# A decoder layer's self attention: the Newton steps of the layer norm's inverse root go from VectorE to GpSimd

## The chip, the cores and the metric

The kernel runs on one core of a Trainium2 chip. The metric is the device time of one execution in microseconds (us), as a median of several runs. Lower is better. The engines are TensorE (PE in the rows, PEld for its weight loads), VectorE (DVE), ScalarE (ACT), GpSimd (POOL) and SyncE (SP, here only a DMA queue).

## The reference, cut to what matters

The reference is one post-norm decoder layer on a batch of 8 sequences of 224 rows of 512: self attention, cross attention and a quantised feed-forward part, each followed by a residual add and a layer norm.

```
x = _layernorm(x + attn(rmsnorm(x)))     # 16 heads of 64, q and k normalised per head, scores soft-clamped by tanh
x = _layernorm(x + xattn(x, ctx))        # 16 heads, context of 750 rows of 384
x = _layernorm(x + ffn(x))
_layernorm(x) = (x - mean) / sqrt(var + 1e-5)      # over the 512 columns of a row
```

The layer norm behind self attention is the part that the change touches. Its inverse root is computed without a square root instruction: an integer shift and subtract give a first guess, and three Newton iterations refine it.

## The kernel before

Self attention takes its 16 heads in two groups of 8 (`g` = 0 and 1), and each group runs over the 8 sequences (`b`). One step of a group is a hand-written order of named pieces on each engine. A piece without a plus sign belongs to sequence b, one with a plus to b+1, one with two to b+2. The engines meet only by semaphores. A group's eight sequences are six steps in a loop, then steps written out; the last sequence of the second group is interleaved with the first pieces of cross attention by lists at the end of the file (`turn` on ACT, DVE and POOL, and a list of its own on PE).

The pieces that matter here are these.

- PE: `S1` to `S3` score pairs of heads, `O0` to `O7` multiply the values of one head by its weights, `Q0 K0 Q1 K1 V0 V1` project the next sequence, `T0` to `T3` transpose q and k, `Y0 Y1` project the output. `O4` waits for the low part of head 4's weights, and so on. `K1` goes to the PSUM bank that `Q0` leaves, so it waits until DVE has scaled `Q0` (line 729). `T0` waits for the scaled q and k of both halves (also line 729). The order on PE around them is: S1 O0 O1 S2 Q0+ O2 O3 K0+ S3 O4 O5 Q1+ O6 O7 K1+ V0+ Y0 T0+.
- ACT: exponentials, the high part `p_hi` of each head's weights (line 599), copies of the sums (lines 607 and 608), squares of projected rows (line 579).
- POOL: `P0` to `P7` subtract the high part from each head's weights, giving `p_lo` (line 392). `B0` to `B3` split the normalised output of a pair of heads into `o_hi` and `o_lo` (lines 398 and 400). Its order: P1 P2 P3 B0 P4 P5 P6 P7 B1 B2 B3, and then P0 of the next sequence.
- DVE: `I0` to `I3` invert the weight sums (`sa_sums`, line 751), `D0` to `D3` normalise the outputs with them (lines 758 and 759) and so free the bank and feed `B0` to `B3`. `HQ0` to `HK1` reduce squares per head (line 708). `N0.x` and `N1.x` are the inverse roots of the head norms, 12 dependent links each, after which q and k are scaled (line 729). `F0` to `F14` are the layer norm of the second group: F0 statistics (lines 778 and 779), F1 aggregation, F2 adds the epsilon, F3 and F4 make the guess (lines 1938 and 1940), F5 to F13 are the nine links of three Newton iterations on [112 x 2] elements, and F14 normalises the two halves of y (line 790), after which SP may store them.

DVE's order in a step ends with Y1, F0, T3+, XT0++, XT1++, F1 to F10, I0+, D0+, F11, F12, HQ0++, F13, F14, I1+, and the next step begins with HK0+, D1, N0.0+ and so on up to N0.11+, then Q0+.

Cross attention's second group has its own layer norm, and there the Newton iterations already run on POOL, in the form that the change brings to self attention: `refine_rsqrt` (lines 1384 to 1388), twelve dependent instructions on [112 x 2] in POOL's queue, between a wait for DVE's guess and a semaphore for which DVE's last link waits (line 1849).

Of the kernel before, what the change touches and what calls it, by code (L numbers as in the profile page):

```python
# [14 lines left out]
ALU = mybir.AluOpType  # L15
# [102 lines left out]
def self_attention(nc, ctx, at, psum, shared, x, norm_w, Wq, Wkv, Wo, q_gamma, k_gamma, acc, x1, ff_weights, ff_sum, ff_mean, ff_scale):  # L118
# [11 lines left out]
    LINKS = 1 + RSQRT_LINKS  # L130
    LN_LINKS = 3 + RSQRT_LINKS
    NW = len(ff_weights)
# [246 lines left out]
    def gpsimd(pool):  # L379
# [317 lines left out]
    def vector(dve):  # L697
# [116 lines left out]
        def values_lo(c, at):  # L814
# [3 lines left out]
            for t in range(2):  # L818
# [1721 lines left out]
```

## Time and profile before

| what | value |
|---|---|
| median of 3 runs | 1896.25 us (1895.83 to 1899.11) |
| the profiled execution | 1895.53 us, its span 1894.0 us |
| busy: PE, DVE, ACT, POOL over the span | 94%, 77%, 62%, 54% |
| self attention's second group, loop and unrolled steps | about 380 to 605 us of the span |
| one step of it | 35.36 us, PE busy 34.48 of them, DVE 30.53, ACT 22.81, POOL 14.25 |
| granted TensorE clock in that step | 1.00 of full speed |

Times in the rows count from the span's start. A row of the timeline is: start, length, engine, line, operation, output <- inputs with shapes, count; a bracket at the end is the idle time of the engine just before and what ended it. Neighbouring instructions of one group are merged ("x2"), and the length is then from the first start to the last end.

### The profile page before, as it was taken

The page shows a single profiled execution, that of the slowest core. Times are in us where ns is not written, and L with a number is a line of the kernel's source. Part 1 is how long each engine was busy: PE and PEld are TensorE (multiplying, and loading weights), DVE is VectorE, ACT ScalarE, POOL GpSimd, SP SyncE. Part 2 cuts the span into 40 slices and gives each one's busy share as a digit, 9 for nine tenths or more (in the row PEclk, how much of TensorE's full clock was granted, in tenths as well). Part 3 has the DMA queues.
Part 4 walks back from the last instruction along what each step waited for, and adds up shares of the span by engine and source line. Part 5 has one row for each costly group of instructions (what it writes and reads, how often), then busy time and mean ns, then how long its engine had stood idle before and what let it go on. Part 6 is the DMA issues. An engine that isn't in the chain of part 4 may idle for free.

```text
span 1894.0 us, 43077 instructions
## 1 busy us (share of the span) xinstructions
PE 1785.3 (94%) x14154; PEld 1492.8 (79%) x14154; DVE 1464.7 (77%) x3382; ACT 1181.4 (62%) x2696; POOL 1024.4 (54%) x1161
## 2 busy tenths in 40 slices
PE   5899998999999899999999999999999999979997
PEld 4777776777777788998998998899999999964443
DVE  5667667788888777787787788878777877778887
ACT  5675777566566565666665666566566656655664
POOL 0343343334434257766766744578778778542554
PEclk9899999999999899999999999999999999989999
DMA  3322233101103334324324333233313331271221
GB/s 121 116 85 72 74 104 107 40 29 39 48 29 120 98 99 127 102 93 144 99 67 144 118 132 91 58 93 91 110 55 107 90 110 47 67 161 41 67 66 61
DMA packets 109574, 166.80 MB, mean 88 GB/s; under 512 B 32488, under 2 KB 67672, under 8 KB 109512
## 3 DMA queue, kind: packets, MB, share of 16 engines
q1 hardware_dynamic: 91016, 129.77, 22.3%
q0 software_dynamic: 14656, 28.92, 5.5%
q10 hardware_dynamic: 3840, 7.34, 1.3%
q8 instruction: 33, 0.54, 0.1%
q14 instruction: 29, 0.24, 0.0%
HBM read 109.25 MB, written 50.46 MB: 84 GB/s over the span
## 4 chain that ended last, share of the span: by engine, by line
PE 58%; DVE 16%; issue 9%; DMA 6%; ACT 5%; POOL 4%; SPq 1%; POOLq 0%; DVEq 0%; ACTq 0%
PE att_ps_P L1524 5%; PE att_ps_SA L1548 5%; PE att_ps_P L1512 4%; PE att_ps_P L1573 3%; PE att_ps_T L1512 3%; PE att_ps_T L451 3%; PE att_ps_O L1512 3%; PE att_ps_T L1524 3%; PE att_ps_P L1562 3%; PE att_ps_O L1524 3%; DVE sa_sums L751 2%; PE att_ps_P L1584 2%; PE att_ps_SB L513 2%; PE att_ps_T L1573 2%; DMA out_dram<-ff_y_out 2%
## 5 line engine op out<-in xcount | busy, mean ns | idle before, releaser
L1360 POOL TENSOR_TENSOR ca_pr<-ca_pr,ca_rec 112x750 f32<-112x750 f32 x256 | 370.1, 1466 | 218.8 <-DVE ca_rec L1799 215.8
L392 POOL TENSOR_TENSOR sa_p_lo<-sa_pr,sa_p_hi 112x448 fp32r<-112x448 f32 x128 | 148.0, 1162 | 330.9 <-ACT sa_p_hi L599 330.9
L1689 ACT ACTIVATE ca_big<-att_ps_P 126x384 fp32r<-126x384 f32 (+1 forms) x256 | 105.7, 448 | 69.2 <-PE att_ps_P L1562 67.8
L751 DVE RECIPROCAL sa_sums<-sa_sums 128x224 f32<-128x224 f32 x64 | 99.2, 1550 | 46.7 <-ACT sa_sums L608 46.3
L1683 ACT ACTIVATE ca_pr<-att_ps_SA,ca_nmax 112x750 f32<-112x750 f32 x128 | 113.6, 888 | 20.0 <-DVE ca_nmax L1795 9.5
L1804 DVE TENSOR_TENSOR ca_big<-att_ps_P,ca_big 126x384 fp32r<-126x384 f32 (+1 forms) x256 | 120.1, 497 | 4.4 <-ACT ca_big L1689 4.1
L1795 DVE TENSOR_REDUCE ca_nmax<-att_ps_SA 112x1 f32<-112x752 f32 x128 | 119.1, 930 | 0.4 <-PE att_ps_SA L1548 0.4
L1795 DVE TENSOR_REDUCE ca_nmax<-att_ps_SB 112x1 f32<-112x752 f32 x128 | 118.9, 929 | 0.0
L1524 PE MATMUL att_ps_P<-ca_w_hi,ca_ct 128*126 128x256 f32 x576 | 118.2, 284 | 0.0
L1683 ACT ACTIVATE ca_pr<-att_ps_SB,ca_nmax 112x750 f32<-112x750 f32 x128 | 113.1, 884 | 0.0
L1573 PE MATMUL att_ps_P<-ca_big,ca_v_st 126*128 126x448 f32 x378 | 90.9, 376 | 8.3 <-DVE ca_big L1804 8.3
L451 PE MATMUL att_ps_T<-sa_w_hi,sa_xt_hi 128*112 128x512 f32 x192 | 82.6, 430 | 16.3 <-DVE sa_qs L729 10.7
L1562 PEld LDWEIGHTS att_ps_P<-att_ident,ca_pr 64*126 64x126 f32 (+1 forms) x1536 | 85.5, 138 | 14.8 <-issue 10.3
L1562 PE MATMUL att_ps_P<-att_ident,ca_pr 48*126 48x48 f32 (+1 forms) x1536 | 92.6, 223 | 4.5 <-DVE ca_q_lo L1778 2.2
L1548 PE MATMUL att_ps_SA<-ca_k_hi,ca_q_hi 64*112 64x376 f32 x256 | 94.3, 368 | 2.2 <-ACT ca_pr L1683 2.2
L1524 PEld LDWEIGHTS att_ps_P<-ca_w_hi,ca_ct 128*126 128x126 f32 x576 | 94.0, 187 | 2.2
L1548 PE MATMUL att_ps_SB<-ca_k_hi,ca_q_hi 64*112 64x376 f32 x256 | 94.0, 367 | 0.0
L1401 POOL TENSOR_SCALAR ca_stage<-ca_stage 128x688 f32<-128x688 f32 x36 | 90.5, 2513 | 3.1
L499 PE MATMUL att_ps_SB<-sa_p_hi,sa_v_hi 112*128 112x224 f32 x256 | 77.5, 303 | 11.5 <-POOL sa_p_lo L392 10.9
L1548 PE MATMUL att_ps_SA<-ca_k_hi,ca_q_lo 64*112 64x376 f32 x256 | 85.3, 333 | 0.0
L1548 PE MATMUL att_ps_SB<-ca_k_hi,ca_q_lo 64*112 64x376 f32 x256 | 85.2, 333 | 0.0
L1548 PE MATMUL att_ps_SA<-ca_k_lo,ca_q_hi 64*112 64x376 f32 x256 | 85.2, 333 | 0.0
(342 smaller groups left out, 6653.5 us busy)
## 6 DMA issues: line engine op xcount, KB each, us to landing
ct_kept<-ca_ct SPq DMA_DIRECT2D x8, 1134.0 KB, 9.2
ca_ct<-ct_kept POOLq DMA_DIRECT2D x8, 1134.0 KB, 8.1
ct_kept<-ca_ct SPq DMA_DIRECT2D x8, 1116.0 KB, 12.0
ca_ct<-ct_kept POOLq DMA_DIRECT2D x8, 1116.0 KB, 10.1
sa_xin<-in_x_dram SPq DMA_DIRECT2D x16, 448.0 KB, 3.8
xt_kept<-ca_xt SPq DMA_DIRECT2D x8, 896.0 KB, 5.3
ca_xt<-xt_kept POOLq DMA_DIRECT2D x8, 896.0 KB, 5.0
ternary<-ca_stage SPq DMA_DIRECT2D x36, 172.0 KB, 1.9
```

Of the source, the lines that this page charges most:

```text
L392: pool.tensor_tensor(p_lo[:, h % NB, :], pr[:, h % NB, :], f32(p_hi[:, h % NB, :]), ALU.subtract).then_inc(p_split, 1)
L451: mm = pe.matmul(ps(u)[0:R, :], xs[:, k, c * R:c * R + R], ws[i][:, k, :], start=(n == 0), stop=(n == len(passes) - 1))
L751: dve.reciprocal(sums[:, p % 2, :], sums[:, p % 2, :]).then_inc(inverted, 1)
L1360: pool.tensor_tensor(w, w, rec[:, h % PB, c:c + 1].to_broadcast([R, S]), ALU.mult).then_inc(norm_done, 1)
L1512: mm = pe.matmul(st(u).bank[:, 0:SH], ws[:, k, p * P:p * P + P], cs[:, k, a * S1:a * S1 + SH], start=(n == 0), stop=(n == len(todo) - 1))
L1524: mm = pe.matmul(st(u).bank[0:J, 0:VC], cs[:, k, J0[j]:J0[j] + J], ws[:, k, vh * VC:vh * VC + VC], start=(n == 0), stop=(n == len(todo) - 1))
L1548: mm = pe.matmul(psum[scores_slot(h)][0:R, BANK * half:BANK * half + SH], qs[of, p, c * R:c * R + R], ks[of, p, half * S1:half * S1 + SH], ...
L1562: mm = pe.transpose(to.bank[0:J, j * width:j * width + width], pr[rows, h % PB, c, J0[j]:J0[j] + J], ident[rows, rows])
L1573: mm = pe.matmul(to.bank[:, 0:2 * N], v_st[0:JN[j], j, h, :], big[0:JN[j], h % 2, j, :, :].rearrange("s l n -> s (l n)"), start=(j == 0), ...
L1683: act.activation(pr[:, h % PB, c, :].rearrange("r (a s) -> r a s", a=2), two_halves(psum[slot]), ACT.Exp, bias=nmax[:, h % PB, c:c + 1], a ...
L1795: dve.tensor_reduce(nmax[:, h % PB, c:c + 1], both, AX.XY, ALU.max, negate=True).then_inc(max_done, 1)
L1804: dve.tensor_tensor(weights_view(h, c, x, True), blocks_view(source.bank, x), f32(weights_view(h, c, x, False)), ALU.subtract).then_inc(so ...
```

## The change

1. The nine Newton links leave DVE. DVE keeps F0 to F4 (statistics, epsilon, guess); the new F5 is the old F14, and it first waits for `rs_done`.
2. POOL gets a piece `L`: it waits for `guess_done`, runs twelve [112 x 2] instructions, each waiting for the one before, and raises `rs_done`. Where DVE fused a multiply and an add in one instruction, POOL uses two. `rs_begun` is raised on the way; nobody in self attention waits for it.
3. In POOL's order the loop body is cut at another place: P1, P2, P3 and B0 of a sequence now stand at the end of the body before. The sequence of instructions is the same in the loop except that L stands between P3 and B0. In the last sequence, B0 moves from behind P5 to ahead of P4, and the last L stands behind B3.
4. In DVE's order, I0 and D0 come right behind F4, then HQ0, then F5, then I1. In the closing list the same is done for the last two sequences: I0 and D0 ahead of the norm's last link for sequence 6, and K00, K01 ahead of it for sequence 7.
5. The variance with epsilon and the scratch tile lie in SBUF instead of PSUM, since POOL works on them.

```diff
-    LN_LINKS = 3 + RSQRT_LINKS
+    LN_LINKS = 5
...
-        ORDER = steps("""P1 P2 P3 B0 P4 P5 P6 P7 B1 B2 B3 P0+""")
+        ORDER = steps("""P4 P5 P6 P7 B1 B2 B3 P0+ P1+ P2+ P3+ L B0+""")
+        rs_chain = Chain(pool, rs_own, 3 * 4)
+
+        def refine_rsqrt(b):
+            rs_chain.step(counter(b, 0, B))
+            pool.wait_ge(guess_done, counter(b, 0, B)(1, 1))
+            pool.sem_inc(rs_begun, 1)
+            for n in range(3):
+                rs_chain.link(pool.tensor_tensor(ln_newton[:, :], mv[:, :, 1], rs[:, :], ALU.mult))
+                rs_chain.link(pool.tensor_tensor(ln_newton[:, :], ln_newton[:, :], rs[:, :], ALU.mult))
+                pool.sem_inc(rs_begun, 1)
+                rs_chain.link(pool.tensor_scalar(ln_newton[:, :], ln_newton[:, :], -0.5, 1.5, ALU.mult, ALU.add))
+                rs_chain.link(pool.tensor_tensor(rs[:, :], rs[:, :], ln_newton[:, :], ALU.mult))
+            pool.sem_inc(rs_done, 1)
...
-            elif link < LN_LINKS:
-                rsqrt_link(dve, link - 3, ln_var, rs[:, :], ln_newton).then_inc(ln_own, 1)
+            elif link == 3:
+                rsqrt_link(dve, 0, mv[:, :, 1], rs[:, :], ln_newton[:, :]).then_inc(ln_own, 1)
+            elif link == 4:
+                rsqrt_link(dve, 1, mv[:, :, 1], rs[:, :], ln_newton[:, :]).then_inc(guess_done, 1)
             else:
+                dve.wait_ge(rs_done, at(1, 1))
                 for c in range(2):
                     dve.tensor_scalar(y[:, c, :], y[:, c, :], mv[:, c, 0:1], rs[:, c:c + 1], ALU.subtract, ALU.mult).then_inc(y_done, 1)
...
-                   V1+ T1+ T2+ G++ Y1 F0 T3+ XT0++ XT1++ F1 F2 F3 F4 F5 F6 F7 F8 F9 F10 I0+ D0+ F11 F12 HQ0++ F13 F14 I1+""")
+                   V1+ T1+ T2+ G++ Y1 F0 T3+ XT0++ XT1++ F1 F2 F3 F4 I0+ D0+ HQ0++ F5 I1+""")
...
-            turn("""P1 P2 P3 P4 P5 B0 P6 B1 P7 B2 B3 N0.0+ ...
+            turn("""P4 P5 P6 B1 P7 B2 B3 L N0.0+ ...
...
-            turn("""E0 w0+ w1+ E1 E2 E3 E4 E5 E6 E7 E8 E9 E10 E11 E12 E13 E14 I0 D0 I1 D1 ... Y1 F0 Q0+ F1 F2 F3 F4 F5 K00+ F6 F7 F8 F9
-                    F10 K01+ F11 F12 F13 F14 M0.0+ ...
+            turn("""E0 w0+ w1+ E1 E2 E3 E4 I0 D0 E5 I1 D1 ... Y1 F0 Q0+ F1 F2 F3 F4 K00+ K01+ F5 M0.0+ ...
```

(The E pieces of the last list are the F pieces of sequence 6, done under another letter.)

## Rows read from the trace of the kernel before

**Rows 1.** What PE waited for, 390 to 620 us: total, times, longest.
```profile
PE att_ps_SB L499 <- POOL sa_p_lo L392: 4.0, 2, 2.2
PE att_ps_T L451 <- DVE sa_qs L729: 3.4, 6, 0.8
PE att_ps_P L468 <- DVE sa_qs L729: 1.6, 6, 0.3
```

**Rows 2.** Timeline of PE in one step: O4, O5, Q1, O6, O7, K1, T0.
```profile
473.50 0.37 PE L499 MATMUL att_ps_SB<-sa_p_hi,sa_v_hi 112*128 112x224 f32 x1
...
474.27 0.27 PE L499 MATMUL att_ps_SB<-sa_p_hi,sa_v_hi 112*128 112x224 f32 x1
...
474.94 0.40 PE L451 MATMUL att_ps_P<-sa_w_hi,sa_xt_hi 128*112 128x512 f32 x1
...
478.27 0.27 PE L499 MATMUL att_ps_SB<-sa_p_hi,sa_v_lo 112*128 112x224 f32 x1
478.62 0.37 PE L499 MATMUL att_ps_SB<-sa_p_hi,sa_v_hi 112*128 112x224 f32 x1
...
480.07 0.48 PE L451 MATMUL att_ps_T<-sa_w_hi,sa_xt_hi 128*112 128x512 f32 x1 [0.52 <-DVE sa_qs L729]
...
488.95 0.41 PE L468 MATMUL att_ps_P<-att_ident,sa_qs 112*128 112x112 f32 x2 [0.29 <-DVE sa_qs L729]
```

**Rows 3.** Timeline of POOL in the same step: P3, B0 (two rows), P4, P5.
```profile
467.66 1.15 POOL L392 TENSOR_TENSOR sa_p_lo<-sa_pr,sa_p_hi 112x448 fp32r<-112x448 f32 x1 [0.63 <-ACT sa_p_hi L599]
469.70 0.56 POOL L398 TENSOR_TENSOR sa_o_hi<-sa_o,att_zero 128x224 fp32r<-128x224 f32 x1 [0.89 <-DVE sa_o L759]
470.34 0.67 POOL L400 TENSOR_TENSOR sa_o_lo<-sa_o,sa_o_hi 128x224 fp32r<-128x224 f32 x1
470.97 1.39 POOL L392 TENSOR_TENSOR sa_p_lo<-sa_pr,sa_p_hi 112x448 fp32r<-112x448 f32 x1
472.55 1.15 POOL L392 TENSOR_TENSOR sa_p_lo<-sa_pr,sa_p_hi 112x448 fp32r<-112x448 f32 x1 [0.19 <-ACT sa_p_hi L599]
```

**Rows 4.** Timeline of DVE in the same step: F4, HQ0, F14, I1.
```profile
465.90 0.16 DVE L1940 TENSOR_SCALAR sa_rs<-att_ps_O 112x2 int32<-112x2 int32 x1
...
469.87 0.69 DVE L708 TENSOR_REDUCE att_ps_O<-sa_sq 112x8 f32<-112x512 f32 x1
...
470.80 1.85 DVE L790 TENSOR_SCALAR sa_y<-sa_y,sa_mv,sa_rs 112x512 f32<-112x512 f32 x2
472.56 1.54 DVE L751 RECIPROCAL sa_sums<-sa_sums 128x224 f32<-128x224 f32 x1
```

**Rows 5.** Timeline of POOL in cross attention: the same Newton pass, first, third and last link.
```profile
1284.84 0.19 POOL L1384 TENSOR_TENSOR ca_newton<-ca_mv,ca_rs 112x2 f32<-112x2 f32 x1 [1.01 <-DVE ca_rs L1940]
...
1285.50 0.19 POOL L1387 TENSOR_SCALAR ca_newton<-ca_newton 112x2 f32<-112x2 f32 x1 [0.20 <-POOL ca_newton L1385]
...
1288.20 0.20 POOL L1388 TENSOR_TENSOR ca_rs<-ca_rs,ca_newton 112x2 f32<-112x2 f32 x1
1288.64 0.67 POOL L1365 TENSOR_TENSOR ca_o<-ca_o,ca_tmp 128x224 f32<-128x224 f32 x1 [0.24 <-POOL ca_rs L1388]
```

**Rows 6.** Timeline of DVE behind that pass: the last link of the norm.
```profile
1289.17 1.24 DVE L1849 TENSOR_SCALAR ca_res<-ca_res,ca_mv,ca_rs 112x512 f32<-112x512 f32 x2
```

**Rows 7.** Timeline of POOL in the last sequence: P2 and P3, P4 and P5.
```profile
609.18 2.23 POOL L392 TENSOR_TENSOR sa_p_lo<-sa_pr,sa_p_hi 112x448 fp32r<-112x448 f32 x2 [4.33 <-ACT sa_p_hi L599]
612.47 2.24 POOL L392 TENSOR_TENSOR sa_p_lo<-sa_pr,sa_p_hi 112x448 fp32r<-112x448 f32 x2 [1.07 <-ACT sa_p_hi L599]
```

**Rows 8.** Timeline of PE in the last sequence: the last matmul of O5.
```profile
616.40 0.27 PE L499 MATMUL att_ps_SB<-sa_p_hi,sa_v_lo 112*128 112x224 f32 x1
```

**Rows 9.** The chain that ended last: start, length, what.
```profile
617.56 0.35 ACT sa_sums L607
...
642.60 1.01 DVE sa_y L790 x2
```

**Rows 10.** Timeline of DVE in the last norm: F4.
```profile
639.56 0.16 DVE L1940 TENSOR_SCALAR sa_rs<-att_ps_O 112x2 int32<-112x2 int32 x1
```

More of the change, by code:

```diff
@@ L265, in self_attention @@
     ln_own = sem("ln_own")
+    guess_done = sem("guess_done")
+    rs_begun = sem("rs_begun")
+    rs_own = sem("rs_own")
+    rs_done = sem("rs_done")
     ff_loaded = [sem(f"ff_loaded{m}") for m in range(NW)]
@@ L410, in step @@
             for name, n in ORDER:
-                if batches[n]:
+                if name == "L":
+                    if g and batches[n]:
+                        refine_rsqrt(b)
+                elif batches[n]:
                     do(name, batches[n][1])
@@ L420, in gpsimd, with last @@
                 step(b, g)
-        return lambda name: do(name, counter(B - 1, GROUPS - 1, B))
+        def last(name):
+            if name == "L":
+                refine_rsqrt(B - 1)
+            else:
+                do(name, counter(B - 1, GROUPS - 1, B))
+        return last
     def tensor(pe):
@@ L772, in layernorm_link @@
             at = counter(b, 0, B)
-            if link:
-                dve.wait_ge(ln_own, at(LN_LINKS, link))
+            if 0 < link < LN_LINKS:
+                dve.wait_ge(ln_own, at(LN_LINKS - 1, link))
             if link == 0:
@@ L784, in layernorm_link @@
             elif link == 2:
-                dve.tensor_scalar(ln_var, mv[:, :, 1], LN_EPS, None, ALU.add).then_inc(ln_own, 1)
-            elif link < LN_LINKS:
-                rsqrt_link(dve, link - 3, ln_var, rs[:, :], ln_newton).then_inc(ln_own, 1)
+                dve.tensor_scalar(mv[:, :, 1], mv[:, :, 1], LN_EPS, None, ALU.add).then_inc(ln_own, 1)
+            elif link == 3:
+                rsqrt_link(dve, 0, mv[:, :, 1], rs[:, :], ln_newton[:, :]).then_inc(ln_own, 1)
+            elif link == 4:
+                rsqrt_link(dve, 1, mv[:, :, 1], rs[:, :], ln_newton[:, :]).then_inc(guess_done, 1)
             else:
+                dve.wait_ge(rs_done, at(1, 1))
                 for c in range(2):
@@ L2453, in _ @@
             ff_first, ff_rest = ff.gpsimd(pool)
-            turn("""P1 P2 P3 P4 P5 B0 P6 B1 P7 B2 B3 N0.0+ N1.0+ N0.1+ N1.1+ N2.0+ N3.0+ N2.1+ N3.1+ B0+ N4.0+ N5.0+""", last, first)
+            turn("""P4 P5 P6 B1 P7 B2 B3 L N0.0+ N1.0+ N0.1+ N1.1+ N2.0+ N3.0+ N2.1+ N3.1+ B0+ N4.0+ N5.0+""", last, first)
             rest(ff_first)
@@ L2484, in _ @@
             last = sa.vector(dve)
-            turn("""E0 w0+ w1+ E1 E2 E3 E4 E5 E6 E7 E8 E9 E10 E11 E12 E13 E14 I0 D0 I1 D1 I2 D2 CT00+ XT0+ w2+ w3+ XT1+ I3 D3
-                    CT01+ w4+ w5+ total CT02+ w6+ CT10+ w7+ Y0 CT11+ CT12+ w8+ w9+ Y1 F0 Q0+ F1 F2 F3 F4 F5 K00+ F6 F7 F8 F9
-                    F10 K01+ F11 F12 F13 F14 M0.0+ M1.0+ K10+ R0.0+ R1.0+ K11+ Q1+ K20+ M0.1+ M1.1+ K21+ R0.1+ R1.1+ Q2+ w10+
+            turn("""E0 w0+ w1+ E1 E2 E3 E4 I0 D0 E5 I1 D1 I2 D2 CT00+ XT0+ w2+ w3+ XT1+ I3 D3
+                    CT01+ w4+ w5+ total CT02+ w6+ CT10+ w7+ Y0 CT11+ CT12+ w8+ w9+ Y1 F0 Q0+ F1 F2 F3 F4 K00+ K01+ F5 M0.0+ M1.0+ K10+ R0.0+ R1.0+ K11+ Q1+ K20+ M0.1+ M1.1+ K21+ R0.1+ R1.1+ Q2+ w10+
                     w11+ T0.0a+ T0.0b+ T1.0a+ T1.0b+ M2.0+ M3.0+ Q3+ V00+ R2.0+ V01+ R3.0+ w12+ V02+ w13+ V03+ T0.1a+ T0.1b+
```

3 lines of the change are left out of this document (1 added, 2 removed).

## The prediction

> **What bounds the kernel now.** I began with the page and the windows view of one step of the second group: PE is busy for 34.5 of a step's 35.4 us, so hardly a microsecond a step is to be won here, and the waits view says what it is. The reader is to see two gates of DVE in it [rows 1]: in each of six steps PE stands for 3.4 / 6 = 0.57 us ahead of K1 and for 1.6 / 6 = 0.27 us ahead of T0, both times for rows scaled at line 729. The third row is POOL's p_lo, and its two waits, 4.0 us together, lie in the last sequence, not in the loop. So in the loop a shorter DVE can give back 0.57 + 0.27 = 0.84 us a step at the very most, and POOL costs PE almost nothing there as yet. What that "nothing" rests on is the next view: the timeline of the four engines over one step, PE in [rows 2], POOL in [rows 3], DVE in [rows 4]. P4 is done at 470.97 + 1.39 = 472.36 and O4 starts at 473.50, so head 4's low part has 1.14 us to spare. P5 is done at 472.55 + 1.15 = 473.70 and O5 starts at 474.27: 0.57 us to spare. O7 has none: it starts 0.35 us after the matmul before it, where the pitch of these matmuls is 0.11 us, so it already waits some 0.24 us.
>
> **What the change takes from DVE.** Nine links of [112 x 2], six ahead of I0 and three around HQ0. F4, an instruction of the same size, took 0.16 us [rows 4], so they are 9 x 0.16 = 1.4 us of DVE's queue a step, and a little more with the gaps between dependent links. It counts only if I1, HK0 and the N0 chain behind them really start earlier, and that is decided by when the new F5 may run.
>
> **What it puts on POOL, and when.** The pass's price has a row: the same twelve instructions on the same shape in cross attention run from 1284.84 to 1288.20 + 0.20 = 1288.40, which is 3.56 us, and POOL's next instruction follows 0.24 us later [rows 5]. L stands behind P3. P3 waits for ACT's high part of head 3, which the change doesn't move, and ends at 467.66 + 1.15 = 468.81 [rows 3]. The guess has been there since about 466.1 [rows 4], so the wait for it costs nothing, and the pass begins one wait and one semaphore increment later, 0.20 us by the gap ahead of line 1387 [rows 5]: 469.0. It ends at 472.6, and B0 starts at 472.8 instead of 469.70, 3.1 us late. That is the step on which everything turns: P3 is the wrong neighbour, because P4 and P5 are due within 5 us of it and B0 must go first.
>
> **The path over POOL and PE.** B0 takes 1.27 us to P4's start (469.70 to 470.97) [rows 3]; in cross attention the instruction behind the pass took 0.67 us, so I allow B0 up to 1.5. P4 then starts at 474.1 to 474.3 and ends 1.15 later at 475.3 to 475.5; P5 ends at 476.4 to 476.7. O4 can't start at 473.50 but at 475.4, and O5 not before 476.5 to 476.7 instead of 474.27: 2.2 to 2.4 us late, and Q1 with it. Of that O7's 0.24, K1's 0.57 and T0's 0.27 are swallowed, as these waits end later anyway: 2.3 - 1.1 leaves 1.1 to 1.4 us a step on this path alone.
>
> **The path over DVE.** F5 stands where the old F14 stood, ahead of I1, and it now waits for the pass: about 472.8 against 470.80, 2.0 us late. Behind it in DVE's queue are I1, HK0, D1 and the N0 chain, back to back up to Q0's scaling, which is K1's gate. F5's own length matters too. Before, the pair took from 470.80 to 472.56, 1.76 us, with POOL in P4; the last sequence's pair took 1.01 with POOL idle [rows 9], and cross attention's pair, which runs beside the same neighbours on POOL as F5 will, took 1.24 [rows 6]. So I1 starts at 474.0 (by the cross attention row) to 474.5 (by the 1.76) instead of 472.56: 1.4 to 2.0 us late, and K1 and then T0 with it. The nine links saved are used up in the wait. The row nearest to the case is cross attention's, so I take 1.5 us a step for the larger of the two paths; they run side by side and don't add.
>
> The pair of line 790 shows two engines in each other's way: 1.85 us beside P4, 1.01 alone, and P4 itself 1.39 instead of 1.15 [rows 3, 4, 9]. The Trainium skill (GPSIMD Engine Reference, Key points) says that GpSimd shares its SBUF interfaces with VectorE, with contention when VectorE works in a two-port mode or reads two SBUF inputs. By that rule moving work of VectorE's to GpSimd also makes the rest meet more often; if F5 met P4 again I would take the upper end, 2.0 us a step, and the sum would be 3 us more. The trace agrees with the rule in the rows just named; it doesn't change which path decides.
>
> **The number of steps.** F and L of sequences 0 to 5 fall into such steps: six, as many as the waits in [rows 1]. 6 x 1.5 = 9.0 us (6.6 to 12.0).
>
> **Sequence 6, in the crossing to cross attention.** P2 and P3 end at 609.18 + 2.23 = 611.41 [rows 7]. The pass follows, 611.6 to 615.2; B0, now ahead of P4, takes 615.4 to about 616.8; P4 ends at 617.9 and P5 at 619.1, where before both were done by 612.47 + 2.24 = 614.71. O5 ended at 616.40 + 0.27 = 616.67 [rows 8] and now starts at 619.1, ending at 619.8 to 620.4 (the upper end if the clock is low, as it was shortly before). ACT's copy of that pair's sums began at 617.56 and is a piece of the chain that ended last [rows 9]; it now begins at 619.9 to 620.4. So 2.3 to 2.9 us, and I take 2.6. The sooner I0 and D0 don't help, since B0 stands behind the pass.
>
> **Sequence 7, the last norm.** DVE's guess ends at 639.56 + 0.16 = 639.7 [rows 10], POOL is idle, and the pass takes 639.9 to 643.5. The closing pair starts at 643.6 instead of 642.60, and it too lies on the chain that ended last [rows 9], ahead of the store that cross attention's next loads queue behind: 1.0 us. Zero if those loads have slack that the chain doesn't show.
>
> **At nothing.** The cut of POOL's loop at another place changes no order in the first group, and P1 to P3 wait for ACT wherever the cut is. SBUF in place of PSUM for the [112 x 2] tiles touches F2 and F3, which are ahead of I0 and no longer than F4's 0.16 us each [rows 4]; even at half that, more or less, DVE has time there, since it must wait for the pass afterwards. The store of y comes 1.4 to 2.0 us later, and y is needed again only by Y0's add, which is behind T0's gate at 488.95 [rows 2], some 16 us after the pair's end: only a delay of that size would use up the cover.
>
> **The sum.** 9.0 + 2.6 + 1.0 = 12.6 us. Against the profiled execution's 1895.53 that is 1908.1; the median of the runs shown is 0.7 higher than that execution, so the forecast for a median is 1908.8.
>
> **The rivals.**
>
> *VectorE's relief decides (faster).* If L were done early enough, F5 would follow HQ0 directly, at 469.87 + 0.69 = 470.6 or sooner [rows 4], K1's wait would vanish and perhaps part of T0's: up to 0.84 x 6 = 5.0 us, so 1891 to 1894. For it speaks that PE does wait for DVE in each step and that DVE is without a pause from its Y1 add to T0's gate. Against it: it needs `rs_done` by 470.6, and P3 alone ends at 468.81. The pass would have to take under 1.8 us, half of what [rows 5] shows. Chance 0.05.
>
> *It is hidden (no change).* The delays on POOL and DVE might meet slack I count wrongly, for example if PE catches up by other pieces, and only the ends remain: 2 to 3 us, 1896 to 1899. Against it: PE has 0.9 us of idle in a step, and P5's slack is 0.57 us against 3 us of delay. Chance 0.07.
>
> *Only the path over POOL counts, and the ends are covered.* 6 x 1.1 with little else: 1902 to 1905. Chance 0.13, and it lies at the lower edge of my range.
>
> *It costs more.* F5 meets P4 again, PE's clock falls to its lower level in the longer pauses of the crossing, and that stretch grows by several us: 6 x 2.0 + 2.9 + 1.0 and 2 to 4 for the clock, 1914 to 1917. The granted clock of the windows around 600 to 650 us is already the lowest of the stage. Chance 0.10.
>
> **How the numbers follow.** The forecast has 0.65: 1905 to 1914 with 6.6 to 12.0 for the steps and 2.3 to 3.9 for the ends. Range 1902 to 1914, which leaves out the rivals of the first two kinds and most of the last. A measurement of this kernel tells 0.2%, 3.8 us, from no change. Faster by more 0.04, within 0.09, slower 0.87.
>
> **What will show it.** Right: in a step of the second group, L's first link 0.2 us behind P3 and 3.56 us long; B0 3.1 us later against P3; new rows for PE at line 499 waiting for p_lo at O4 and O5, some 2.3 us a step; the DVE pair of line 790 preceded by idle time ended by POOL; step length near 36.9 us. K1's wait stays or grows although DVE is less busy by at least 1.4 us a step. Wrong: step length 34.5 to 35.4 and no wait at O4. The prediction fails if POOL's pass is far from 3.56 us here, or if P4 and P5 are not what PE waits for.

## The result, and the profile after

The changed kernel takes 1914.49 us (median of 4 runs, 1913.83 to 1918.05) against 1897.24 us (4 runs beside it, 1895.83 to 1899.11): ratio 1.009, 95% interval 1.0074 to 1.0106. It is slower by 17.25 us; 12.6 us were forecast, and the time lies 0.5 us above the range given. One execution of the filled version below ran at a granted clock of 0.65, took 2466 us and is left out of its ratio.

Where PE waits, first: the view that answers to [rows 1], 390 to 640 us (total, times, longest).

```profile
PE att_ps_SB L524 <- POOL sa_p_lo L408: 16.4, 13, 3.0
```

Both gates of DVE are gone from the list, and what is left is POOL's p_lo. The timeline of PE in one step (the one whose P3 starts at 473.86) shows where; the rows are the last of S3, the first of O4 and of O5, the last two of O5, the first two of Q1, two of Q1 behind the turn of the clock, and the first of O6, K1 and T0. [rows 2] has most of them for the kernel before.

```profile
479.51 0.27 PE L507 MATMUL att_ps_SA<-sa_q_hi,sa_k_lo 64*112 64x224 f32 x2
481.52 0.37 PE L524 MATMUL att_ps_SB<-sa_p_hi,sa_v_hi 112*128 112x224 f32 x1 [1.75 <-POOL sa_p_lo L408]
...
482.63 0.37 PE L524 MATMUL att_ps_SB<-sa_p_hi,sa_v_hi 112*128 112x224 f32 x1 [0.18 <-POOL sa_p_lo L408]
...
483.23 0.41 PE L524 MATMUL att_ps_SB<-sa_p_lo,sa_v_hi 112*128 112x224 f32 x1
483.45 0.41 PE L524 MATMUL att_ps_SB<-sa_p_hi,sa_v_lo 112*128 112x224 f32 x1
483.66 0.63 PE L476 MATMUL att_ps_P<-sa_w_hi,sa_xt_hi 128*112 128x512 f32 x1
484.09 0.63 PE L476 MATMUL att_ps_P<-sa_w_lo,sa_xt_hi 128*112 128x512 f32 x1
...
486.59 0.40 PE L476 MATMUL att_ps_P<-sa_w_lo,sa_xt_hi 128*112 128x512 f32 x1
486.82 0.39 PE L476 MATMUL att_ps_P<-sa_w_hi,sa_xt_lo 128*112 128x512 f32 x1
...
487.74 0.27 PE L524 MATMUL att_ps_SB<-sa_p_hi,sa_v_hi 112*128 112x224 f32 x1
...
489.08 0.40 PE L476 MATMUL att_ps_T<-sa_w_hi,sa_xt_hi 128*112 128x512 f32 x1
...
497.64 0.41 PE L493 MATMUL att_ps_P<-att_ident,sa_qs 112*128 112x112 f32 x2
```

Two things are to be seen. PE stands for 1.75 us ahead of O4, as forecast. And behind that pause the distance from one 128x512 matmul to the next is 0.43 us (483.66 to 484.09) instead of 0.23 (486.59 to 486.82): the clock fell from 2.4 to 1.2 GHz at about 483.1, since the last two matmuls of O5 are already 0.22 us apart where the pitch was 0.11, and it came back at about 486.4. The fall is there in all six steps. Q1 takes 487.74 - 483.66 = 4.08 us, where it took 477.72 - 474.94 = 2.78 us before. The windows view, 400 to 600 us, says the same for all steps (columns: time, then busy us of PE, PEld, DVE, ACT and POOL, the granted clock, DMA); the first row is of the kernel before.

```profile
400.00:600.00 200.00, 194.57 (x1251) 151.41 (x1249) 173.00 (x467) 124.74 (x283) 80.05 (x91) 1.00 0.14 43
```

```profile
400.00:600.00 200.00, 188.05 (x1168) 147.02 (x1168) 155.91 (x389) 121.17 (x276) 89.19 (x156) 0.95 0.13 39
```

POOL and DVE in the same step, answering to [rows 3] and [rows 4]: P3, first and last link of the pass, B0, then P4 to P6 in one row; below it the guess's last instruction (F4), HQ0, the pair F5 and I1.

```profile
473.86 1.16 POOL L408 TENSOR_TENSOR sa_p_lo<-sa_pr,sa_p_hi 112x448 fp32r<-112x448 f32 x1 [0.64 <-ACT sa_p_hi L624]
474.98 0.20 POOL L399 TENSOR_TENSOR sa_ln_newton<-sa_mv,sa_rs 112x2 f32<-112x2 f32 x1
...
478.34 0.19 POOL L403 TENSOR_TENSOR sa_rs<-sa_rs,sa_ln_newton 112x2 f32<-112x2 f32 x1
478.85 0.73 POOL L414 TENSOR_TENSOR sa_o_hi<-sa_o,att_zero 128x224 fp32r<-128x224 f32 x1 [0.32 <-POOL sa_rs L403]
479.66 0.72 POOL L416 TENSOR_TENSOR sa_o_lo<-sa_o,sa_o_hi 128x224 fp32r<-128x224 f32 x1
480.34 3.34 POOL L408 TENSOR_TENSOR sa_p_lo<-sa_pr,sa_p_hi 112x448 fp32r<-112x448 f32 x3
```

```profile
472.11 1.14 DVE L1968 TENSOR_SCALAR sa_rs<-sa_ln_newton 112x2 int32<-112x2 int32 x1
...
475.56 0.69 DVE L733 TENSOR_REDUCE att_ps_O<-sa_sq 112x8 f32<-112x512 f32 x1
478.62 1.25 DVE L818 TENSOR_SCALAR sa_y<-sa_y,sa_mv,sa_rs 112x512 f32<-112x512 f32 x2 [2.36 <-POOLq L404]
479.78 1.54 DVE L776 RECIPROCAL sa_sums<-sa_sums 128x224 f32<-128x224 f32 x1
```

The pass takes 478.53 - 474.98 = 3.55 us, and from P3's start to B0's it is 4.99 us instead of 2.04. A step, measured between equal rows of two steps, has 37.88 us instead of 35.36: +2.52. Over the whole second group, from P3 of sequence 0 (398.09, before 396.94) to P0 of sequence 7 (618.45, before 602.59), it is 220.36 - 205.65 = 14.7 us.

The ends: Y0's add of the last sequence, and the last pair of the norm, with the kernel before in the first fence.

```profile
633.26 0.69 DVE L768 TENSOR_TENSOR sa_y<-att_ps_SB,sa_res 112x512 f32<-112x512 f32 x1 [1.84 <-PE att_ps_SB L513]
```

```profile
652.06 0.69 DVE L793 TENSOR_TENSOR sa_y<-att_ps_SB,sa_res 112x512 f32<-112x512 f32 x1 [0.93 <-PE att_ps_SB L538]
...
662.38 1.00 DVE L818 TENSOR_SCALAR sa_y<-sa_y,sa_mv,sa_rs 112x512 f32<-112x512 f32 x2 [1.48 <-POOLq L404]
```

P2 of sequence 7 starts at 625.54 (609.18 in [rows 7]), so from there to Y0's add it is 26.52 us instead of 24.08: +2.4, forecast 2.6. From Y0's add to the pair it is 10.32 instead of 9.34 [rows 9]: +1.0, forecast 1.0. Between the two stretches, from P0 to P2 of sequence 7, lie 7.09 us instead of 6.59, +0.5; cross attention's first weights are on the chain there and land 7.3 us behind their issue instead of 6.8. 14.7 + 0.5 + 2.4 + 1.0 = 18.6 us. The two profiled executions are 22.5 us apart, since the changed one is 3.6 us above its median and the one of before 1.7 below the median beside it; of the 3.9 us left, 1.15 lie ahead of P3 of sequence 0 and the rest behind the last norm; their cause is open.

The +2.4 agree with the forecast in part by luck. The copy of sums that the forecast followed starts 637.26 - 625.54 = 11.72 us behind P2, where it was 617.56 - 609.18 = 8.38: 3.3 us late, not 2.3 to 2.9; O4 and O5 ran at 1.2 GHz behind a pause of 3.01 us and took 2.9 us together. Up to Y0's add 0.9 us of it were caught up.

### The profile page after: what moved, and what is told of

It reads as the page before. It is cut to its first block, busy times and chain, and to the rows that moved or that the text cites. A ratio compares the mean times of both kernels' runs of the same rounds, so it can differ in the third digit from the quotient of the medians.

```text
span 1916.5 us, 43151 instructions
## 1 busy us (share of the span) xinstructions
PE 1791.7 (93%) x14128; PEld 1500.8 (78%) x14154; DVE 1455.7 (76%) x3310; ACT 1181.6 (62%) x2696; POOL 1041.8 (54%) x1257
## 4 chain that ended last, share of the span: by engine, by line
PE 52%; issue 15%; DVE 9%; POOL 9%; DMA 8%; ACT 5%; SPq 1%; POOLq 1%; DVEq 0%; ACTq 0%
PE att_ps_SA L1576 5%; PE att_ps_P L1552 5%; PE att_ps_P L1540 4%; PE att_ps_P L1601 3%; PE att_ps_O L1540 3%; PE att_ps_T L1540 3%; DMA ca_ct<-ct_kept 3%; PE att_ps_T L1552 3%; PE att_ps_P L1590 2%; POOL sa_p_lo L408 2%; PE att_ps_O L1552 2%; PE att_ps_P L1612 2%; PE att_ps_T L476 2%; PE att_ps_T L1601 2%; DMA out_dram<-ff_y_out 2%
```

## The experiments

Each was timed beside the kernel before on the same chip. Medians of the kernel before were 1895.6 us beside the first four runs below, 1897.6 beside the two smaller passes, Q1 ahead of O4 with the pass, and the split pass, 1896.7 beside the four from the pass in GpSimd's idle time to the filling without a pause, and 1896.9 beside the pair moved alone and Q1 ahead of O4 without the pass. "Step" is the length of one step of the second group in the profile.

**GpSimd's pass alone.** VectorE keeps its code; GpSimd does twelve instructions of the same kind on tiles of its own, in the changed kernel's order.

```
-        ORDER = steps("""P1 P2 P3 B0 P4 P5 P6 P7 B1 B2 B3 P0+""")
+        ORDER = steps("""P4 P5 P6 P7 B1 B2 B3 P0+ P1+ P2+ P3+ L B0+""")
...
+                rs_chain.link(pool.tensor_tensor(own_newton[:, :], own_var[:, :], own_rs[:, :], ALU.mult))
```

> VectorE as before the change, with all its Newton links; GpSimd has the twelve instructions behind P3 too, on tiles of its own, and nobody waits for their result. Theory: the loss of a step comes over GpSimd, which hands head 4's and 5's low parts to TensorE about 2 us late; TensorE then pauses and runs at its lower clock for some 3 us behind the pause. It expects O4's pause of 1.7 to 1.8 us, the low clock behind it, a step of 37.5 to 38 us instead of 35.36 and 1909 to 1914 us. Rival 1, the loss comes from VectorE's wait for rs_done: no pause ahead of O4 that costs anything in the end, a step of 35.4 to 36 and 1896 to 1900 us.

Measured: 1916.33 us, ratio 1.0101 (1.0087 to 1.0114), step 37.7 us, granted clock 0.95. The timeline of PE, O4:

```profile
481.28 0.56 PE L523 MATMUL att_ps_SB<-sa_p_hi,sa_v_hi 112*128 112x224 f32 x1 [1.99 <-POOL sa_p_lo L413]
```

The whole loss is there with none of VectorE's waits for GpSimd: I1 starts 4.23 us behind P3 here, earlier than in the kernel before. The path over POOL is enough for it. The pass took 4.02 us and not 3.55, and B0 to P4 1.25 and not 1.49, so O4 comes 0.2 us later than in the changed kernel.

The steps of this trace aren't equal: 36.54, 37.72, 37.70, 39.21 and 38.11 us, with a pause of 1.97 to 2.00 us ahead of O4 in each. The rows show the first and the fourth: O4's first matmul and two neighbours of Q1 behind it.

```profile
407.02 0.37 PE L523 MATMUL att_ps_SB<-sa_p_hi,sa_v_hi 112*128 112x224 f32 x1 [1.97 <-POOL sa_p_lo L413]
...
409.13 0.39 PE L475 MATMUL att_ps_P<-sa_w_lo,sa_xt_hi 128*112 128x512 f32 x1
409.36 0.39 PE L475 MATMUL att_ps_P<-sa_w_hi,sa_xt_lo 128*112 128x512 f32 x1
```

```profile
518.98 0.56 PE L523 MATMUL att_ps_SB<-sa_p_hi,sa_v_hi 112*128 112x224 f32 x1 [1.99 <-POOL sa_p_lo L413]
...
522.11 0.63 PE L475 MATMUL att_ps_P<-sa_w_lo,sa_xt_hi 128*112 128x512 f32 x1
522.54 0.63 PE L475 MATMUL att_ps_P<-sa_w_hi,sa_xt_lo 128*112 128x512 f32 x1
```

In the first step the matmuls behind the pause stay 0.23 us apart. The clock didn't fall, and the step is 1.18 us longer than the 35.36 before: that is the price of the delay alone. In the fourth the slow stretch lasts from O4 to 525.5, some 6.5 us, and the step is 2.67 us longer than the first. One kernel, the same pause, and the step's length goes with the stretch at 1.2 GHz.

**VectorE's relief alone.** No pass, no Newton iteration; the pair waits for the guess only.

```
-                dve.wait_ge(rs_done, at(1, 1))
+                dve.wait_ge(guess_done, at(1, 1))
```

> The Newton iterations are left out altogether: the norm is scaled with the first guess. VectorE has the new short order, GpSimd has no pass. All theories expect a gain, since this is the most that VectorE's relief can be worth: TensorE's waits for VectorE ahead of K1 (0.57 us) and T0 (0.27 us) go, a step of 34.5 to 34.9 us, 1891 to 1894 us. If the relief is worth nothing even then, 1896 to 1898 us and a step of 35.3.

Measured: 1896.88 us, ratio 1.0008 (0.9998 to 1.0018), step 35.27 us. A miss: 1.4 us less on VectorE gave back 0.09. The timeline of DVE (the guess's last instruction, the pair, I1) and of POOL (P2, P4) says why.

```profile
465.34 1.17 DVE L1968 TENSOR_SCALAR sa_rs<-sa_ln_newton 112x2 int32<-112x2 int32 x1
...
469.55 2.28 DVE L818 TENSOR_SCALAR sa_y<-sa_y,sa_mv,sa_rs 112x512 f32<-112x512 f32 x2
471.75 1.54 DVE L776 RECIPROCAL sa_sums<-sa_sums 128x224 f32<-128x224 f32 x1
```

```profile
465.33 1.16 POOL L408 TENSOR_TENSOR sa_p_lo<-sa_pr,sa_p_hi 112x448 fp32r<-112x448 f32 x1 [2.54 <-ACT sa_p_hi L624]
...
470.21 1.34 POOL L408 TENSOR_TENSOR sa_p_lo<-sa_pr,sa_p_hi 112x448 fp32r<-112x448 f32 x1
```

An instruction on 112 x 2 elements took 1.17 us and ended with P2, and the pair ended 0.3 us behind P4. What the nine links had cost went into waiting beside POOL: 1.0 us at the guess's last instruction and 0.4 at the pair (2.28 instead of 1.85), so VectorE's busy time between 400 and 600 us is 173.4 us, where it was 173.0 before.

**VectorE's wait alone.** As in the last run, without pass and Newton links, but the pair also waits for the low part of head 4 of the next sequence, so it is late and GpSimd isn't.

```
+                if not isinstance(b, int) or b < B - 1:
+                    dve.wait_ge(p_split, counter(b, 1, B, 1)(HG, 5))
```

> As the run without iterations, but VectorE's last link of the norm waits for head 4's low part of the next sequence, which is ready at about the moment at which rs_done came, while GpSimd has no pass in its way. So only VectorE is late. The theory (GpSimd's lateness and the clock) expects no pause ahead of O4, and ahead of K1 1.5 to 1.8 us instead of 0.57: a step of 36.2 to 36.6 and 1901 to 1905 us if TensorE's clock stays up behind that pause. If the clock falls behind any pause of this length, 2.5 us a step and 1911 or more. Rival 1 (VectorE's wait carries the loss) expects 1911 to 1915 us too, but with the full clock in the rows.

Measured: 1903.33 us, ratio 1.004 (1.0027 to 1.0053), step 35.85 us, clock 0.99. PE, K1 and T0:

```profile
480.58 0.49 PE L476 MATMUL att_ps_T<-sa_w_hi,sa_xt_hi 128*112 128x512 f32 x1 [0.96 <-DVE sa_qs L754]
...
489.47 0.41 PE L493 MATMUL att_ps_P<-att_ident,sa_qs 112*128 112x112 f32 x2 [0.30 <-DVE sa_qs L754]
```

The path over VectorE exists, and costs 0.5 us a step here. K1's wait is 0.96 us and not the 1.5 to 1.8 expected, because this edit holds VectorE back less than the pass does: I1 starts 5.21 us behind P3, 0.31 later than in the kernel before, where the changed kernel has 5.92. So the run doesn't price that path at its full length. Its sixth step comes nearer: there the pair met P5 and took 1.84 us, I1 starts 6.04 us behind P3, K1 waits 1.96 us, the clock is low for some 3.4 us behind it, and the step is 37.73 us instead of 35.41. By that one step (2.3 us) the path over VectorE, left to itself, might cost nearly as much as the path over POOL; no run tests it. In the changed kernel K1 and T0 don't wait at all, so it is hidden there. The six steps add up to 4.8 us more than before, the medians are 7.7 apart, and the profiled execution was the fastest of the five; the rest isn't explained.

**Filling the pause.** The changed kernel with six useless 128x512 matmuls between S3 and O4, into a bank that is free until Q1 writes it.

```
                     do(name, batches[n][1])
+                    if name == "S3" and g and batches[1]:
+                        keep_busy(batches[1][1])
```

> The changed kernel, and TensorE does six useless 128x512 matmuls into Q1's free bank between S3 and O4 in the second group, about 1.4 us in the pause that it has there (1.4 us more work a step in all, whose result is overwritten). Theory: the granted clock stays at full speed behind the pause, O5 and Q1 lose their extra 1.6 us, of which K1's gate gives about 1.3 back: a step of 36.4 to 36.9 us instead of 37.88, 1904 to 1909 us. If the clock has nothing to do with the pause, the same 1914 us or up to 8 us more.

Measured: 1909.11 us, ratio 1.0066 (1.0053 to 1.0079), step 36.55 us, clock 1.00. PE at O4 and O5:

```profile
479.07 0.37 PE L529 MATMUL att_ps_SB<-sa_p_hi,sa_v_hi 112*128 112x224 f32 x1 [0.20 <-POOL sa_p_lo L408]
480.18 0.37 PE L529 MATMUL att_ps_SB<-sa_p_hi,sa_v_hi 112*128 112x224 f32 x1 [0.18 <-POOL sa_p_lo L408]
```

PE does more and the step is 1.33 us shorter. O4 comes no earlier (7.70 us behind P3, in the changed kernel 7.66); what went is the stretch at 1.2 GHz. T0 now waits 0.26 to 0.28 us for VectorE again, so without the low clock the two paths end close together.

**Two iterations, and one.** The pass with `range(2)` and `range(1)` for `range(3)`, and the count of links to match.

> The changed kernel with two of the three Newton iterations in GpSimd's pass (the iterate is less exact, so the outputs differ a little; nothing else is left out). The pass should take 2.35 us instead of 3.5, B0 start 1.2 us earlier and P4 end 0.6 to 0.8 us after the end of S3, where it now is 1.75 us late. Theory A (the delay in front of O4 and the lower TensorE clock behind it are two terms, and the clock term comes only with a long pause): PE pauses 0.5 to 0.8 us at O4, the granted clock of the loop stays at 0.99 to 1.00, and the step is 35.5 to 35.9 us, that is 1896 + 1 to 4 = 1897 to 1900 us. Theory B (the loss is proportional to the delay, with no separate clock term): two thirds of the loss of the step stay, 37.0 us a step, and 1907 to 1909 us. The smaller loss of the ends (2.4 and 1.0 us, each less one iteration of 1.14 us) is in both.

Measured: 1898.17 us, ratio 1.0002 (0.9993 to 1.0012), step 35.36 us, clock 1.00.

```profile
470.55 0.37 PE L524 MATMUL att_ps_SB<-sa_p_hi,sa_v_hi 112*128 112x224 f32 x1 [0.54 <-POOL sa_p_lo L408]
```

> The changed kernel with one of the three Newton iterations in GpSimd's pass (less exact outputs again). The pass takes 1.15 to 1.2 us, B0 starts about 0.6 us later than in the kernel before, and P4 ends at about 473, inside the 1.14 us that O4 has to spare. Both theories: no pause at O4 and O5, clock 1.00, step 35.2 to 35.4 us, 1895 to 1898 us. If the step is still longer by more than 0.3 us, something besides the length of the pass costs time (the wait for the guess, the order of B0 and P4, F5 behind HQ0).

Measured: 1896.07 us, ratio 0.9995 (0.9983 to 1.0008), step 35.00 us, clock 1.00, no wait for p_lo in the steps.

So the loss isn't proportional to the pass: one iteration gives -0.36 us a step, two 0.0, three +2.5. From two to three, 1.2 us of POOL's time, 1.2 us go into the delay of O5 that nothing swallows any more and 1.3 into the clock.

**Q1 ahead of O4**, first with the pass, then in the kernel before.

```
-S3 O4 O5 Q1+ O6 O7 K1+
+S3 Q1+ O4 O5 O6 O7 K1+
```

> The changed kernel with PE's order S3 Q1 O4 O5 O6 O7 K1 instead of S3 O4 O5 Q1 O6 O7 K1: Q1 needs nothing of GpSimd and takes 2.78 us, so it stands in the pause of 1.75 us. Clock theory: no pause at O4, no fall of the clock, O4 to O7 back to back behind Q1 as far as the high and low parts of heads 6 and 7 allow it; what stays is VectorE's late gate of K1 and T0. Step 35.8 to 36.5 us (kernel before 35.36, changed kernel 37.88), granted clock 0.99 to 1.00, 1900 to 1904 us. Rival (the delay itself is the whole loss, wherever PE stands): PE waits at O6, O7 and K1 for as much as it did at O4 and O5, step 37 us or more, 1909 us or more.

> The kernel before with PE's order S3 Q1 O4 O5 O6 O7 K1, in both groups. If the order alone costs (ScalarE copies the sums of O4 and O5 ahead of the high part of head 7, P7 stands behind it on GpSimd, and O7 needs it), PE waits about 1.9 us at O7 in every step, the clock falls behind that, and the time is 1915 us or more. If it costs only together with GpSimd's pass, the step stays within 0.5 us of 35.36 and the time within 1894 to 1900 us.

Measured: 1926.02 us, ratio 1.0153 (1.0137 to 1.0169), step 37.5 us with the pass; 1920.68 us, ratio 1.012 (1.0103 to 1.0137), step 37.5 us without it. A miss. The second run says that the order costs by itself, so the first tells nothing of the pass. From the run without the pass, the timelines of ACT (the first copy of the sums of O4 and O5, head 7's high part), POOL (P7) and PE (O7, and K1 behind it):

```profile
491.01 0.36 ACT L607 ACTIVATE sa_sums<-att_ps_SB 64x224 f32<-64x224 f32 x1 [1.93 <-PE att_ps_SB L499]
...
491.76 0.58 ACT L599 ACTIVATE sa_p_hi<-sa_pr 112x448 fp32r<-112x448 f32 x1
```

```profile
492.42 1.13 POOL L392 TENSOR_TENSOR sa_p_lo<-sa_pr,sa_p_hi 112x448 fp32r<-112x448 f32 x1 [2.11 <-ACT sa_p_hi L599]
```

```profile
493.60 0.37 PE L499 MATMUL att_ps_SB<-sa_p_hi,sa_v_hi 112*128 112x224 f32 x1 [1.96 <-POOL sa_p_lo L392]
...
494.68 0.63 PE L451 MATMUL att_ps_T<-sa_w_hi,sa_xt_hi 128*112 128x512 f32 x1
495.11 0.63 PE L451 MATMUL att_ps_T<-sa_w_lo,sa_xt_hi 128*112 128x512 f32 x1
```

With O4 and O5 behind Q1, ScalarE's sums come late, the high part of head 7 stands behind them in its queue, P7 behind that, and PE meets the same kind of pause at O7, with the same fall of the clock behind it.

**The pass split.** One iteration behind P3, two behind P5 of the next step, the pair behind K0's scaling.

```
+        ORDER = steps("""P4 P5 M P6 P7 B1 B2 B3 P0+ P1+ P2+ P3+ L B0+""")
...
+I2 N0.11+ Q0+ K0+ F5 D2 I3
```

> The pass split up and the pair moved: GpSimd does one iteration behind P3 (0.89 us of idle time there) and the other two behind P5 of the next step (2.36 us of idle time there in the kernel before); VectorE's closing pair of the norm moves from ahead of I1 to behind the scaling of Q0 and K0 in the next step, behind K1's gate. If the place of the pass is what costs, then P4 ends about 0.5 us later than before and within O4's slack, P6 and P7 come 0.5 to 0.7 us late, O7 0.45 us late, and K1's wait of 0.57 and T0's of 0.27 us are swallowed or gone, since I1 starts 1.2 us earlier: step 34.9 to 35.3 us, no pause over 0.6 us, clock 1.00. With about 1 us of loss in the last norm: 1893 to 1897 us. If GpSimd's pass costs wherever it stands (contention with VectorE, P6 and P7 late), the step is 35.6 us or more and the time 1899 us or more.

Measured: 1903.24 us, ratio 1.0029 (1.0017 to 1.0042), step 35.9 us, clock 1.00. A miss in the step: no wait for p_lo, but one for T0's rows.

```profile
495.46 0.41 PE L503 MATMUL att_ps_P<-att_ident,sa_qs 112*128 112x112 f32 x2 [1.21 <-DVE sa_qs L764]
```

From Q0's scaling to the last scaling ahead of T0 VectorE hasn't a pause, and a pair of 0.99 us put into that stretch comes out as 0.9 us more wait.

**The pass where GpSimd idles.** All twelve instructions behind B3 of the next step, the pair behind the last scaling of K1's rows, Y0's add behind V1.

```
+        ORDER = steps("""P4 P5 P6 P7 B1 B2 B3 M P0+ P1+ P2+ P3+ B0+""")
...
+Q1a+ K1a+ Q1b+ K1b+ F5 T0+ V0+ V1+ Y0 T1+
```

> The whole pass of twelve instructions moved to where GpSimd idles: behind B3 of the next step (idle for 10 us there), the closing pair on VectorE behind the last scaling of the Q1 and K1 rows (1.16 us of idle time there), Y0's add one place later (behind V1), and the guess's intermediate back in PSUM. In the crossing the pass of sequence 6 stands between B2 and B3 (3.95 us idle), its pair behind D3. If place alone decides, there is no wait for p_lo in the steps, I1 starts when ScalarE's sums are there (4.24 us behind P3's start instead of 4.90), and the step is 34.8 to 35.1 us, clock 1.00: 1892 to 1896 us, the last norm still costing 1.0. If moving the pair towards T0 costs as in the split version (its pair lay wholly on T0's path), step 35.6 us or more and 1899 us or more.

Measured: step 35.02 us, clock 1.00, but 1903.3 us, ratio 1.004 (1.0025 to 1.0054). The step came out as expected, the total didn't. POOL's pass (first and last link) and DVE's pair, then the waits of PE, 390 to 640 us:

```profile
484.97 0.20 POOL L402 TENSOR_TENSOR sa_ln_newton<-sa_mv,sa_rs 112x2 f32<-112x2 f32 x1
...
488.34 0.20 POOL L406 TENSOR_TENSOR sa_rs<-sa_rs,sa_ln_newton 112x2 f32<-112x2 f32 x1
```

```profile
488.62 1.00 DVE L829 TENSOR_SCALAR sa_y<-sa_y,sa_mv,sa_rs 112x512 f32<-112x512 f32 x2
```

```profile
PE att_ps_P L1536 <- DVE ca_ct L1820: 4.1, 1, 4.1
PE att_ps_P L1521 <- DMA ca_xin<-x: 3.9, 1, 3.9
```

The full pass costs next to nothing in a step if it stands here: the run with only the pair moved has 34.84. The loss is in the crossing: the store of sequence 5 now stands late in SP's queue, and cross attention's first loads behind it. The first weights, issued at 598.13, land 10.69 us later, where it was 6.8 us before. That this is the whole of the loss wasn't tested.

**Guess in PSUM, without and with the pass.** `ln_guess = norms[:, 4 * HN:4 * HN + 2]` for the guess's intermediate, as in the kernel before.

> As the version without pass and without Newton iterations (only the first guess, so the norm is not exact), but the guess's intermediate in PSUM as in the kernel before. There the last instruction of the guess, SBUF to SBUF, took 1.17 us beside P2, and the pair 2.28 us beside B0 and P4. Port theory: an instruction of VectorE's that goes from SBUF to SBUF waits for the end of GpSimd's instruction, one that reads PSUM doesn't: the guess's last instruction takes 0.16 us again, D0 and B0 come 1.0 us earlier, the pair meets less of P4 and takes 1.2 to 1.7 us, I1 starts at the time of ScalarE's sums, step 34.9 to 35.1 us (35.27 without PSUM), 1893 to 1896 us. Rival (the 1.17 us are a property of the instruction and not of where its source lies): 1.17 us stay, step 35.27, 1897 us.

Measured: 1894.9 us, ratio 0.9997 (0.9985 to 1.0008), step 35.03 us (35.27 with SBUF). DVE's instruction and POOL's P2 beside it:

```profile
464.60 0.16 DVE L1969 TENSOR_SCALAR sa_rs<-att_ps_O 112x2 int32<-112x2 int32 x1
```

```profile
464.58 1.16 POOL L409 TENSOR_TENSOR sa_p_lo<-sa_pr,sa_p_hi 112x448 fp32r<-112x448 f32 x1 [2.54 <-ACT sa_p_hi L625]
```

0.16 us beside P2 where SBUF to SBUF took 1.17. The pair still took 2.12 us, not the 1.2 to 1.7 expected: it meets P4 all the same.

> The changed kernel with nothing else altered than the guess's intermediate in PSUM instead of SBUF. The last instruction of the guess should take 0.16 instead of 1.14 us, with I0, D0 and HQ0 1.0 us earlier. The prediction put this placement at nothing, since VectorE has to wait for the pass anyway: then the pair starts at the same distance from P3, the step stays at 37.8 to 37.9 us, and the time at 1912 to 1916 us. If it counts after all (the guess or B0's source being late), the step is shorter by up to 1.0 us and the time lies near 1908 to 1910 us.

Measured: 1911.71 us, ratio 1.009 (1.0072 to 1.0108), step 37.53 us (37.88). The pair starts 4.76 us and I1 5.92 us behind P3's start in both kernels, so VectorE gained nothing, as the prediction had it. The 0.35 us are most likely the clock's: PE's second matmul of O4 already slows down here (0.36 us, then one every 0.21), and the slow stretch covers O5's wait of 0.18, while in the changed kernel it begins only within O5. The first step of this trace has no fall behind its pause of 1.77 us, as in the run with GpSimd's pass alone, and is 36.58 us long.

**The filling without a pause.** The same six matmuls in the kernel before.

> Control for the version with filling matmuls: the kernel before with the same six useless 128x512 matmuls (1.4 us a step) between S3 and O4. No pause there to hide them in. O4 to K1 come 1.4 us later, of which K1's wait of 0.57 and T0's of 0.27 us may swallow a part: step 35.9 to 36.8 us (35.36 without), clock 1.00, 1899 to 1905 us. If the matmuls were of use to the clock by themselves, and not only in the pause, the step would be about 35.4 us or less, 1896 us.

Measured: 1898.54 us, ratio 1.0012 (1.0000 to 1.0024), step 35.44 us, clock 1.00: 0.08 us more for 1.4 us of work. PE has no wait left between 390 and 590 us, so what K1, T0 and the small gaps at O4 to O7 had left idle took it in. A smaller cost than expected, and it gives the filled version its meaning: its 1.19 us over the kernel before are the late O5 and, at T0, VectorE, hardly the filling. The first step of the run with GpSimd's pass alone says the same without any filling: 1.18.

**Only the pair moved.** The kernel before, Newton links on VectorE, GpSimd untouched; the pair behind the last scaling of K1's rows (Z), Y0's add behind V1; sequences 5 and 6 as before.

```
+Q1a+ K1a+ Q1b+ K1b+ Z T0+ V0+ V1+ Y0 T1+
```

> The kernel before, all Newton links left on VectorE and GpSimd untouched; only the closing pair of the norm moved in the steps of the second group, from ahead of I1 to behind the last scaling of K1's rows in the next step (1.16 us of idle time there), with Y0's add one place later; sequences 5 and 6 keep the pair where it was. If the place of the pair is what VectorE can give back, I1 starts 4.24 us behind P3 (when ScalarE's sums are there) instead of 4.90, K1's wait of 0.52 to 0.57 us goes, and the step is 35.0 us (35.36 before) in five steps: 1894 to 1896 us, ratio 0.999. If relief of VectorE needs the Newton links gone as well, the step stays at 35.2 to 35.4 us.

Measured: step 34.84 us (35.36), but 1895.88 us, ratio 0.9992 (0.998 to 1.0004). DVE, I1:

```profile
470.19 1.55 DVE L751 RECIPROCAL sa_sums<-sa_sums 128x224 f32<-128x224 f32 x1 [1.13 <-ACT sa_sums L608]
```

I1 now waits for ScalarE's sums, 4.24 us behind P3's start (465.95), and K1 waits in one step only (0.7 us). The step is 0.52 us shorter, more than with any work taken from VectorE (0.36 at most). Over six steps that is 3 us at most, and a measurement of this kernel doesn't tell it from none.

## Why the prediction was wrong, and where it was right

**Right.** GpSimd's pass: 3.56 us forecast, 3.55 found. B0 3.1 us late: 4.99 - 2.04 = 2.95. B0 up to 1.5 us: 480.34 - 478.85 = 1.49. O5 2.2 to 2.4 us late: measured from P3's start it is at 8.77 us instead of 6.61, 2.16. The path over POOL and PE: 1.1 to 1.4 us a step. Where the clock stays up, the delay costs 1.19 (filled) and 1.18 (first step with GpSimd's pass alone). The last norm 1.0 for 1.0. The crossing 2.4 for 2.6, in part by luck, as said above. Six steps.

**The step that failed is the sum for the loop, "I take 1.5 us a step for the larger of the two paths"; it leaves TensorE's clock out.** It was 2.52 us. The prediction weighed the clock only in the crossing, among the costs of a rival. The trace shows it in every step, behind the pause of 1.75 us ahead of O4: 1.2 GHz for about 3.3 us, and Q1 alone 1.30 us longer. The filled version takes the pause away and not the delay, and 1.33 us a step go; the control without a pause shows that the filling does no good of its own. The unequal steps of the run with GpSimd's pass alone say it a second time, with no edit between them. Six times 1.33 are 8.0 us. The forecast of 9.0 for the loop took the delay 1.9 us too high (6 x 1.19 = 7.1) and the clock 8 us too low; one error hid part of the other.

The Trainium skill (TensorE: Matmul & The Clock Gate, Part 1) says that the clock isn't a matter of voltage or boost: throttled is the default, and activity releases it. The traces agree as far as they go: in the steps, pauses of 1.7 to 2.0 us have such a stretch behind them, except for the first step of two runs (1.97 and 1.77 us), and behind pauses of 0.96 us (VectorE's wait alone) and of 0.54 us (two iterations) there is none.

**The path over VectorE was mis-sized and isn't the one that ends last.** I1 is 5.92 us behind P3's start instead of 4.90, so 1.0 us late and not 1.4 to 2.0: the pass began 0.2 us sooner, and the pair started 0.1 us behind it. The run with GpSimd's pass alone, where this path doesn't exist, lost all the same. That doesn't make it harmless: in the filled version, where the clock stays up, T0 waits for VectorE again, so there the two paths end within 0.3 us of each other.

**"At nothing" for SBUF in place of PSUM was right in the time and wrong in the reason.** It was said that the instructions aren't longer than 0.16 us; the guess's last one takes 1.14. It is hidden because VectorE waits for the pass anyway. Where there is no pass to wait for it costs: 35.27 against 35.03 us a step.

**The rival "VectorE's relief decides".** Its ceiling of 0.84 us a step isn't contradicted: the filling went into 1.3 us of idle time, of which K1's and T0's waits are the 0.8. But less work on VectorE doesn't reach it. Without any Newton link 0.09 us came back, 0.33 with the guess in PSUM besides, and with the pair moved and all links kept 0.52.

**The rivals for more.** "It costs more" named 1914 to 1917 us, where the time fell, but for other reasons: F5 met no P4 (1.25 us), and the crossing was as forecast. "It is hidden" fails, since the pass alone costs 1.01%. "Only the path over POOL counts" had the path right, but priced it without the clock, at 1902 to 1905 us, and its covered ends cost 3.4 us.

**Open.** Why the clock falls at O4's first or second matmul in one kernel, within O5 in another and in two steps not at all, with the same pause ahead. What the path over VectorE would cost alone. And the fixed version of the pass in GpSimd's idle time, with the crossing left as it was, wasn't tried; by the step lengths it would win 2 us at most and lose 1.0 again in the last norm.

## What to carry to other kernels

Price a new pause of a tuned TensorE twice: once as the delay that reaches the end, and once as what the matmuls behind it cost at the lower clock. Where a pause of nearly 2 us comes back in every step of a loop, the second price can be as large as the first. If the steps of one trace differ in length, compare them: it is a control that costs nothing. Before you move work to another engine, look for the place first: the same twelve instructions cost 2.5 us a step behind P3 and next to nothing behind B3, and moving two instructions within VectorE's own queue shortened the step more than taking nine away. A place is free only if the stores and loads that hang on it are too; follow them through SP's queue to the end of the stage.

## What the runs showed of the hardware

An instruction of VectorE's from SBUF to SBUF on 112 x 2 elements took 1.14 to 1.17 us when GpSimd was in P2 (1.15 us), and ended with it (472.11 + 1.14 = 473.25 against 472.07 + 1.15 = 473.22). The same one with its source in PSUM took 0.16 us beside the same P2. The pair of 112x512 took 1.00 us with GpSimd idle, 1.24 to 1.25 with B0 beside it, and 2.12 and 2.28 with P4. The Trainium skill (SBUF — State Buffer, "SBUF: two separate sides") calls the pair of ports that the two engines share an exclusive lock, held for a whole instruction, and not a split of bandwidth. The trace agrees for the small instruction: what counts is when GpSimd's ends, not how much VectorE has to move. It goes the other way too: with GpSimd's pass alone, two of its [112 x 2] instructions beside VectorE's pair took 0.46 and 0.38 us instead of 0.20. And it isn't so for every instruction from SBUF to SBUF: VectorE's reciprocal on 128 x 224 took its usual 1.54 us beside P3, and P3 its usual 1.16 (473.16 and 473.86).
